# A one-core macaron layer: softplus on one activation table set, its last sum on GpSimd in the scans, and two batches of a layer norm on ScalarE

## The chip, the core and the metric

The kernel runs on one core of one Trainium2 chip. The core has TensorE (PE: matrix products; PEld is its weight load), VectorE (DVE), ScalarE (ACT), GpSimd (POOL) and SyncE (SP), which here only issues DMAs. The engines have a queue of instructions each and wait for each other by semaphores. The metric is the device time of one execution in microseconds; lower is better. Before the change the median of three runs is 441.34 us (440.18 to 441.75).

## The reference

Everything is float32. The input `x` has 4 batches of 512 tokens with 256 features.

```
x = x + 0.5 * ffn(layernorm(x))      # 8 experts, the best one per token, plus a shared expert
x = x + ssm(layernorm(x))            # a selective state space model
x = x + 0.5 * ffn(layernorm(x))      # the same weights again

ssm(x):  dt_x, B, C = split(x @ W_x.T, [64, 80])
         dt = softplus(dt_x @ W_dt.T + b_dt)
         for each of 16 states n, along the 512 tokens:
             h = exp(dt * A[:, n]) * h + dt * B[:, n] * x
             y += h * C[:, n]
         return y + x * D
```

The change concerns the middle line: how `softplus(z) = max(z, 0) + ln(1 + exp(-|z|))` is computed, and, beside the scans, the third `layernorm`.

## The kernel before

The features lie on the partitions: `[128, 2, 512]` is one batch, with 2 halves of 128 features. The program runs through the first ffn (to about 110 us), then projections and softplus of batch 0 (to 142.8 us), then 64 scans, four batches of 16 states (to 329.4 us), and then the second ffn. `s = 16 b + n` numbers the scans, and each engine has its own loop `scan(b)` over `n`, written out by hand; nothing reorders instructions. What a scan needs and gives:

- ACT makes `decay(s)`, `exp(dt * A)`, into `da` (L663), up to 3 scans ahead (`ahead`, AHEAD = 3). It waits for scan s - 4, since `da` and `hs` have RING = 4 buffers.
- The input term `dt * x * B` is made in one of two ways. For 42 of the 64 states ACT (`outer`, L679) and DVE (`outer`, L1405) multiply `dtx_t` by a column of B and PE turns the result into a PSUM bank (`turn_dbx`, L1030); the table BY_DVE gives how many of the 4 token tiles are DVE's, in 20 states at least one. For the other 22 states PE multiplies `dtx_t` by diagonal matrices of B (L1037). ACT reads B from `b_t` in SBUF, DVE reads it from `B_T` in the PSUM bank `Y`.
- DVE runs the scan itself (L1421): `da` from SBUF, the input term from PSUM, `hs` to SBUF.
- POOL multiplies `hs` by C into `gs` (L523, one product for each scan), and PE adds the products up in PSUM (`add`, L1054). In PE's loop `turn_dbx(s + 2)` stands ahead of `add(s - 1)`.
- After scan 1 of the next batch DVE adds the finished sum to `x_sb` (`add_y`, L1457). It waits for the `add` of the last state of its batch, and statistics of the third layer norm follow it (L1177). This is the narrow place between two batches.

Softplus of batch b + 1 is worked into the loop of batch b, on all engines: `project` (PE, L983), `project_copy` (ACT, L630), `project_z` (PE, L1003, one half of the features at a time, both into the PSUM bank `T`), `project_abs` (ACT: |z| and, L637, max(z, 0)), `project_exp` (ACT, L641), `project_u` (ACT, L650: 1 + w, with w = exp(-|z|)), `project_w` (DVE, L1370: the rounding error of 1 + w), `project_ln` (ACT, L657: ln(1 + w), with a table load before it and one after it, L663), `project_dt` (DVE, L1381 and L1384: two sums), `turn_dt` (PE, L1014), `project_dtx` (DVE, L1390). `project_bt` turns B (PE, L994) and copies it to SBUF (DVE, L1361). Batch 0 does the same ahead of the scans.

The third layer norm of batch b - 1 is worked into the loop of batch b as well: `rstd_of(2, b - 1)` on POOL, then four `normalise` instructions, on POOL (L469) for batches 0 and 1 and on ACT (L686) for batch 2; ACT takes a bias of -mean * rstd that POOL makes in `shift`. Batch 3's are on DVE, after the scans.

## Time and profile before

| | us |
|---|---|
| median of 3 runs | 441.34 |
| the profiled execution | 441.44 |
| its span, first to last instruction | 439.6 |
| PE busy in the span | 402.4 (92%) |
| DVE busy | 329.5 (75%) |
| POOL busy | 281.1 (64%) |
| ACT busy | 275.0 (63%) |

The 1.84 us between the span and the execution's time lie outside the first and last instruction. The granted TensorE clock is 0.996 of full speed over the span, so matrix products keep one price throughout. The shares are averages over stages with different limits; in the scans DVE, ACT and POOL are all busy most of the time, and the views below cut the span at the three `add_y` instructions (197.57, 244.19 and 289.39 us), so that one row is about one batch.

A row of the timeline has the start in us, the busy time in us, the engine, the line, the operation, output<-input, and in brackets how long the engine stood idle ahead of it and what ended that. A row of grouped instructions has the count, the busy sum in us and the mean in ns.

### The profile page before, as it was taken

What the parts mean: (1) busy time and instruction counts of PE and PEld (TensorE: products, weight loads), DVE (VectorE), ACT (ScalarE), POOL (GpSimd) and SP (SyncE); (2) the same over time, 40 slices, a digit from 0 to 9 for tenths busy, and PEclk for the clock granted to TensorE, in tenths of its full rate; (3) what the DMA queues carried; (4) which work ended last, traced back from release to release, by engine and by line L of the source; (5) the groups of instructions that cost most, each with busy time, mean ns of one, the idle gap of its engine ahead of it and who ended that gap; (6) DMA issues with size and microseconds to landing.
All of it is one profiled execution on the core that took longest, in us unless ns stands there. A gap on an engine that the chain in (4) does not pass through costs nothing. (4 is left out here: it accounts for less than half of the span.)

```text
span 439.6 us, 8329 instructions
## 1 busy us (share of the span) xinstructions
PE 402.4 (92%) x2716; PEld 278.4 (63%) x2716; DVE 329.5 (75%) x518; ACT 275.0 (63%) x501; POOL 281.1 (64%) x216
## 2 busy tenths in 40 slices
PE   6899899999996899899989997989999899899995
...
GB/s 250 385 179 264 48 54 167 284 174 101 204 10 91 73 82 180 81 144 106 186 75 118 141 176 73 115 157 92 121 72 0 172 107 120 99 118 135 111 60 48
DMA packets 50808, 56.84 MB, mean 129 GB/s; under 512 B 16329, under 2 KB 35597, under 8 KB 50768
## 3 DMA queue, kind: packets, MB, share of 16 engines
...
## 5 line engine op out<-in xcount | busy, mean ns | idle before, releaser
L523 POOL TENSOR_TENSOR gs<-hs,c_sb 128x1024 f32<-128x1024 f32 x63 | 148.3, 2380 | 18.7 <-DVE hs L1421 11.4
L1421 DVE TENSOR_TENSOR_SCAN hs<-da,bank 128x1024 f32<-128x1024 f32 x64 | 144.1, 2273 | 4.1 <-PE bank L1030 2.1
L663 ACT ACTIVATE da<-dt_sb,a_neg 128x511 f32<-128x511 f32 x128 | 84.5, 713 | 2.4 <-DVE dt_sb L1384 1.2
L1054 PE MATMUL bank<-ident,gs 128*128 128x128 f32 x504 | 66.3, 275 | 7.5 <-POOL gs L523 5.9
L1054 PEld LDWEIGHTS bank<-ident,gs 128*128 128x128 f32 x504 | 55.9, 141 | 12.1 <-POOL gs L523 9.8
L679 ACT ACTIVATE dbx_t<-dtx_t,h_sb 128x256 f32<-128x256 f32 x145 | 62.1, 498 | 1.6 <-DVE dtx_t L1390 1.4
L879 PE MATMUL bank<-xnT,w_gu 128*128 128x512 f32 x112 | 50.8, 601 | 0.0
L1030 PE MATMUL bank<-ident,dbx_t 128*128 128x128 f32 x336 | 44.2, 274 | 6.8 <-DVE hs L1421 4.1
L477 POOL DMA_INDIRECT da<-rows,row_token x29 | 30.6, 1055 | 29.7 <-DVE row_token L1292 21.2
L1030 PEld LDWEIGHTS bank<-ident,dbx_t 128*128 128x128 f32 x336 | 37.5, 141 | 12.2 <-DVE hs L1421 5.9
L591 ACT ACTIVATE th<-bank,da 128x256 f32<-128x256 f32 x36 | 17.0, 473 | 43.1 <-PE bank L918 30.4
L918 PE MATMUL bank<-w_gu,tt 128*128 x72 | 35.6, 616 | 3.2 <-ACT tt L596 2.2
L498 POOL DMA_INDIRECT token_out<-y_sb,row_token x18 | 19.0, 1056 | 29.2 <-DVE y_sb L1338 26.3
L477 POOL DMA_INDIRECT da<-rows,row_half x14 | 14.7, 1054 | 35.5 <-DVE row_token L1297 27.2
L1328 DVE TENSOR_TENSOR h_sb<-th,bank 128x256 f32<-128x256 f32 x36 | 15.1, 420 | 28.0 <-ACT th L591 27.9
L915 PE MATMUL bank<-w_gu,tt 128*32 x72 | 34.3, 598 | 1.4 <-ACT tt L596 1.4
L879 PEld LDWEIGHTS bank<-xnT,w_gu 128*128 128x128 f32 x112 | 21.0, 194 | 22.4 <-issue 22.3
L915 PE MATMUL bank<-dtx_t,tt 128*32 128x512 f32 x72 | 34.3, 598 | 0.0
L574 ACT ACTIVATE hs<-bank 128x512 f32<-128x512 f32 x10 | 6.0, 597 | 40.0 <-PE bank L879 34.6
L596 ACT ACTIVATE tt<-bank 128x512 f32<-128x512 f32 (+1 forms) x40 | 22.1, 553 | 13.6 <-PE bank L933 12.3
L498 POOL DMA_INDIRECT out<-y_sb,row_token x18 | 19.8, 1098 | 16.1 <-DVE y_sb L1341 8.2
L562 ACT ACTIVATE xnT<-bank 128x512 f32<-128x512 f32 x24 | 13.9, 590 | 17.3 <-PE bank L807 17.2
...
## 6 DMA issues: line engine op xcount, KB each, us to landing
...
```

What stands on the lines that cost most here:

```text
L477: nc.gpsimd.indirect_dma_start(out=xr[:, u, lo:hi], out_offset=None, in_=source, in_offset=bass.IndirectOffsetOnAxis(ap=row, axis=0), boun ...
L498: nc.gpsimd.indirect_dma_start(out=rows_back, out_offset=bass.IndirectOffsetOnAxis(ap=row_token[:, TILE[j]:TILE[j] + 1], axis=0), in_=y_sb ...
L523: nc.gpsimd.tensor_tensor(gs[:, s % 2], hs[:, s % RING], c_sb[:, s % RING].unsqueeze(1).to_broadcast([P, KC, L]), ALU.mult).then_inc(sc_g, 1)
L596: nc.scalar.activation(tt[:, (j + 1) % 2, lo:hi], T[:, lo * P:hi * P].rearrange("p (a t) -> p a t", t=P), ACT.Copy).then_inc(ff_tpc, 1)
L663: nc.scalar.activation(da[:, s % RING, k, 1:L], dt_sb[:, k, seq(s // N)][:, 1:L], ACT.Exp, scale=a_neg[:, k, s % N:s % N + 1]).then_inc(sc ...
L679: step = nc.scalar.activation(plain_buffer(s)[:, i, :], dtx_t[:, b % 2, i, :], ACT.Copy, scale=b_t[:, b, i, n:n + 1])
L879: last = nc.tensor.matmul(shared_banks(r, b, fo)[h], w_gu[:, k, SHARED, h * F + fo * P:h * F + (fo + 1) * P], xnT[:, k, b * L:(b + 1) * L] ...
L915: last = nc.tensor.matmul(H[j % 2][part, :], tt[:, j % 2, 2 + k, part], gu_part(i, g)[:, k, :] if g else w, start=(k == 0), stop=(k == KC ...
L918: last = nc.tensor.matmul(H[j % 2][:, :], tt[:, j % 2, 2 + k], w, start=(k == 0), stop=(k == KC - 1))
L1030: mm = nc.tensor.transpose(DBX[s % 2][:, k, i * P:(i + 1) * P], plain_buffer(s)[:, i, k * P:(k + 1) * P], ident[:])
L1054: mm = nc.tensor.matmul(YA[k][:, i * P:(i + 1) * P], products[:, k, i * P:(i + 1) * P], ident[:], start=(s % N == 0 and i == 0), stop=(s % ...
L1421: nc.vector.tensor_tensor_scan(hs[:, s % RING].rearrange(flat), da[:, s % RING].rearrange(flat), DBX[s % 2][:, :, :].rearrange(flat), 0.0, ...
```

## The change

Softplus: `project_u` becomes one ScalarE instruction over both halves that gives -(1 + w); it writes to SBUF (`neg_u`: half of `dtx_t` for batch 0, `y_sb` for the others) and no longer to PSUM. DVE adds 1 and w to it (`project_rest`, one instruction with both inputs in SBUF), then takes the larger of that and z + b_dt, which it reads from PSUM itself (`project_max`, two instructions); ScalarE's max(z, 0) goes. The last sum, with ln(1 + w), is one instruction (`project_dt`): on DVE for batch 0, on GpSimd in the scans. ScalarE loads the table set `natural_log_exp_and_others` ahead of the scans, so that Exp and Ln change no set; a load now stands ahead of the first Tanh in batch 3.

Banks: the two halves of z, and of `turn_dt`, go to `T` and `Y`, where both went to `T` before. `Y` also holds `B_T`, so `project_z` of the second half waits for the copy of B to SBUF, `project_bt` moves ahead, and DVE's `outer` reads `b_t` in SBUF in place of `B_T` in PSUM. `project_dtx` is one instruction in the scans.

Layer norm: for batches 0 and 1 `normalise` goes from GpSimd to ScalarE (n = 6 to 9), with a `shift` on GpSimd each.

```diff
...
-            return YA[k] if b == 0 else T
+            return (YA if b == 0 else (T, Y))[k]
+
+        def neg_u(b):
+
+            return dtx_t[:, 1].rearrange("p (k a) d -> p k (a d)", k=KC) if b == 0 else sg_h
...
+            def project_dt(b):
+                pool.wait_ge(pj_ln, b + 1)
+                pool.wait_ge(pj_max, KC * (b + 1))
+                nc.gpsimd.tensor_tensor(dt_sb[:, :, seq(b)], log_w, neg_u(b), ALU.add).then_inc(pj_dt, 1)
...
+                    if b < BATCH - 1 and n == 6 + int(b == 0):
+                        project_dt(b + 1)
...
                     if b > 0 and n == 3:
                         rstd_of(2, b - 1)
-                    if b == BATCH - 1 and n == 3:
+                    if b > 0 and n == 3:
                         shift(b - 1)
-                    if 0 < b < BATCH - 1 and 5 <= n < 5 + LT:
-                        normalise(2, b - 1, (n - 5,))
...
                 nc.scalar.activation(w_exp[:, k], pj_bank(b, k), ACT.Abs, bias=b_sb[:, k:k + 1]).then_inc(pj_abs, 1)
-                nc.scalar.activation(dt_sb[:, k, seq(b)], pj_bank(b, k), ACT.Relu, bias=b_sb[:, k:k + 1]).then_inc(pj_max, 1)
...
-            def project_u(b, k):
-
-                if k == 0:
-                    act.wait_ge(pj_exp, b + 1)
-                    act.wait_ge(pj_max, KC * (b + 1))
+            def project_u(b):
+
...
-                nc.scalar.activation(pj_bank(b, k), w_exp[:, k], ACT.Identity, bias=1.0).then_inc(pj_u, 1)
+                    act.wait_ge(pj_dt, b)
+                nc.scalar.activation(neg_u(b), w_exp[:], ACT.Identity, bias=neg_one[:, 0:1], scale=-1.0).then_inc(pj_u, 1)
...
                         project_exp(b + 1)
-                        project_u(b + 1, 0)
+                        project_u(b + 1)
                     if 0 < b < BATCH - 1 and n == 4 + late:
                         project_ln(b + 1)
                     if b == 0 and n == 15:
                         project_copy(2)
-                    if not more and 6 <= n < 6 + LT:
+                    if b > 0 and 6 <= n < 6 + LT:
                         normalise(b - 1, n - 6)
...
-            nc.scalar.preload_act_table(ACT.Exp)
+            nc.scalar.preload_act_table_set(EXP_LN)
...
             project_exp(0)
+            project_u(0)
             project_ln(0)
             shared_gate(0, 3, 1)
+            nc.scalar.preload_act_table_set(EXP_LN)
             act.wait_ge(a_ready, 2)
-            act.wait_ge(pj_dt, KC)
+            act.wait_ge(pj_dt, 1)
...
                 if b == 0:
                     pe.wait_ge(sh_hidden, 6)
                 else:
-                    pe.wait_ge(sc_dve, states_by("dve", N * (b - 1) + 4 + 3))
+                    pe.wait_ge(pj_btc, b)
...
                 if b > 0 and k > 0:
-                    pe.wait_ge(pj_max, KC * b + k)
+                    pe.wait_ge(pj_btc, b + 1)
...
-                pe.wait_ge(pj_dt, KC * (b + 1))
-                if b > 0 and h > 0:
-                    pe.wait_ge(pj_dtx, 2 * b + h)
-                dst = YA[h] if b == 0 else T
+                pe.wait_ge(pj_dt, b + 1)
+                dst = pj_bank(b, h)
...
-                    if more and n == 3:
+                    late = (2, 1, 0, 0)[b]
+                    if more and n == late:
                         project_bt(b + 1)
...
-                    if more and n - int(b == 0) in (8, 10):
-                        turn_dt(b + 1, (n - 8) // 2)
+                    if more and n - int(b == 0) in (8, 9):
+                        turn_dt(b + 1, n - int(b == 0) - 8)
...
-            def project_w(b, k):
-
-                if k == 0:
-                    dve.wait_ge(pj_exp, b + 1)
-                    dve.wait_ge(pj_max, KC * (b + 1))
-                if b > 0:
-                    dve.wait_ge(pj_u, KC * (b - 1) + k + 1)
-                    nc.vector.scalar_tensor_tensor(out=pj_bank(b, k), in0=pj_bank(b, k), scalar=1.0, in1=w_exp[:, k],
-                                                   op0=ALU.subtract, op1=ALU.subtract).then_inc(pj_rest, 1)
-                    return
-                nc.vector.tensor_scalar(pj_bank(b, k), w_exp[:, k], 1.0, -1.0, ALU.add, ALU.add).then_inc(pj_w, 1)
-                dve.wait_ge(pj_w, KC * b + k + 1)
-                nc.vector.tensor_tensor(pj_bank(b, k), w_exp[:, k], pj_bank(b, k), ALU.subtract).then_inc(pj_rest, 1)
...
-            def project_dt(b, k):
-
-                dve.wait_ge(pj_ln, b + 1)
-                dve.wait_ge(pj_rest, KC * b + k + 1)
-                nc.vector.tensor_tensor(pj_bank(b, k), log_w[:, k], pj_bank(b, k),
-                                        ALU.add if b == 0 else ALU.subtract).then_inc(pj_sum, 1)
-                dve.wait_ge(pj_sum, KC * b + k + 1)
-                nc.vector.tensor_tensor(dt_sb[:, k, seq(b)], pj_bank(b, k), dt_sb[:, k, seq(b)], ALU.add).then_inc(pj_dt, 1)
-
...
+            def project_rest(b):
+
+                dve.wait_ge(pj_u, b + 1)
+                nc.vector.scalar_tensor_tensor(out=neg_u(b), in0=neg_u(b), scalar=1.0, in1=w_exp[:],
+                                               op0=ALU.add, op1=ALU.add).then_inc(pj_rest, 1)
+
+            def project_max(b):
+
+                dve.wait_ge(pj_rest, b + 1)
+                for k in range(KC):
+                    nc.vector.scalar_tensor_tensor(out=neg_u(b)[:, k], in0=pj_bank(b, k), scalar=b_sb[:, k:k + 1], in1=neg_u(b)[:, k],
+                                                   op0=ALU.add, op1=ALU.max).then_inc(pj_max, 1)
+
+            def project_dt():
+
+                dve.wait_ge(pj_ln, 1)
+                dve.wait_ge(pj_max, KC)
+                nc.vector.tensor_tensor(dt_sb[:, :, seq(0)], log_w, neg_u(0), ALU.add).then_inc(pj_dt, 1)
...
+            def project_dtx(b):
+
+                halves = ((0, 1), (1, 2)) if b == 0 else ((0, 2),)
+                for lo, hi in halves:
+                    dve.wait_ge(pj_tp, 2 * b + hi)
+                    src = pair[3 if b == 0 else 1][:, lo:hi].rearrange("p h (i d) -> p (h i) d", d=D)
+                    nc.vector.tensor_tensor(dtx_t[:, b % 2, 2 * lo:2 * hi], src, xn[:, LT * b + 2 * lo:LT * b + 2 * hi, :],
+                                            ALU.mult).then_inc(pj_dtx, hi - lo)
...
+                    dve.wait_ge(pj_btc, b + 1)
                 nc.vector.tensor_tensor(plain_buffer(s)[:, LT - mine:, :], dtx_t[:, b % 2, LT - mine:, :],
-                                        B_T[:, b, LT - mine:, n:n + 1].to_broadcast([P, mine, D]), ALU.mult).then_inc(sc_dve, 1)
+                                        b_t[:, b, LT - mine:, n:n + 1].to_broadcast([P, mine, D]), ALU.mult).then_inc(sc_dve, 1)
...
-                    if more and n == 4:
+                    late = int(b == 0)
+                    if more and n == (3, 2, 1)[b]:
                         project_bt(b + 1)
-                    late = int(b == 0)
-                    if more and n in (5 + late, 7 + late):
-                        project_w(b + 1, (n - 5) // 2)
-                    if more and n in (6 + late, 8 + late):
-                        project_dt(b + 1, (n - 6) // 2)
-                    if more and n in (10 + late, 12 + late):
-                        project_dtx(b + 1, (n - 10) // 2)
+                    if more and n == 5 + late:
+                        project_rest(b + 1)
+                    if more and n == 6 + late:
+                        project_max(b + 1)
+                    if more and n == 11 + late:
+                        project_dtx(b + 1)
...
```

What stands in a queue now, at three places.

PE in batch 0, from the addition of the first product to the transposition that scan 5 needs (`bank2` is `T`, `bank0` and `bank4` are the banks of the input term, `bank6` is the sum). Before:

```order
L1054 MATMUL bank6<-ident,gs 128x128 x8
L983 MATMUL bank2<-xnT,w_x 96x512 x2
L1030 MATMUL bank0<-ident,dbx_t 128x128 x8
L1054 MATMUL bank6<-ident,gs 128x128 x8
L1003 MATMUL bank2<-th,w_dt 128x512
L994 MATMUL bank2<-ident,th 128x16 x4
L1030 MATMUL bank4<-ident,dbx_t 128x128 x8
```

And now:

```order
L1066 MATMUL bank6<-ident,gs 128x128 x8
L997 MATMUL bank2<-xnT,w_x 96x512 x2
L1008 MATMUL bank2<-ident,th 128x16 x4
L1042 MATMUL bank0<-ident,dbx_t 128x128 x8
L1066 MATMUL bank6<-ident,gs 128x128 x8
L1017 MATMUL bank2<-th,w_dt 128x512
L1042 MATMUL bank4<-ident,dbx_t 128x128 x8
```

`project_bt` (L994, now L1008) stood behind the transposition for scan 4 and behind `project_z`; now it is the first thing behind `project(1)`, and the transposition for scan 4 (bank0) waits behind it. `project_bt` waits for ScalarE's copy of what `project(1)` gave. In batch 2 it stands in the same place behind `project(3)`, ahead of the transposition for scan 34 and of the last `add` of batch 1, for which `add_y(1)` waits.

DVE in batch 1, from scan 20 (n = 4) to scan 24; rows with `hs<-da` are scans. Before:

```order
L1421 SCALAR_TENSOR_TENSOR hs<-da,bank0 128x1024
L1361 COPY h_sb<-bank2 128x64
L1421 SCALAR_TENSOR_TENSOR hs<-da,bank4 128x1024
L1370 SCALAR_TENSOR_TENSOR bank2<-bank2,w_exp 128x512
L1421 SCALAR_TENSOR_TENSOR hs<-da,bank0 128x1024
L1381 TENSOR_TENSOR bank2<-tt,bank2 128x512
L1384 TENSOR_TENSOR dt_sb<-bank2,dt_sb 128x512
L1421 SCALAR_TENSOR_TENSOR hs<-da,bank4 128x1024
L1370 SCALAR_TENSOR_TENSOR bank2<-bank2,w_exp 128x512
L1405 TENSOR_TENSOR dbx_t<-dtx_t,bank2 128x256
L1421 SCALAR_TENSOR_TENSOR hs<-da,bank0 128x1024
```

And now, with B's copy ahead of scan 19 (no row here):

```order
L1432 SCALAR_TENSOR_TENSOR hs<-da,bank0 128x1024
L1432 SCALAR_TENSOR_TENSOR hs<-da,bank4 128x1024
L1378 SCALAR_TENSOR_TENSOR y_sb<-y_sb,w_exp 128x1024
L1432 SCALAR_TENSOR_TENSOR hs<-da,bank0 128x1024
L1385 SCALAR_TENSOR_TENSOR y_sb<-bank2,b_sb,y_sb 128x512 x2
L1432 SCALAR_TENSOR_TENSOR hs<-da,bank4 128x1024
L1416 TENSOR_TENSOR dbx_t<-dtx_t,h_sb 128x256
L1432 SCALAR_TENSOR_TENSOR hs<-da,bank0 128x1024
```

Two `project_w` and four sums became one `project_rest` over 1024 elements, with both inputs in SBUF, and two `project_max`. The `outer` (`dbx_t<-dtx_t`) read `bank2` (`B_T`); that of state 26 here reads `h_sb`, where `b_t` lies, now.

POOL in batch 1, from the statistics' rstd on. Before:

```order
L454 TENSOR_SCALAR var_eps<-mv 128x4
L455 TENSOR_TENSOR rstd<-var_eps,neg_half 128x4
L523 TENSOR_TENSOR gs<-hs,c_sb 128x1024 x2
L469 TENSOR_SCALAR xn_no<-x_sb,mv,rstd 128x256
L523 TENSOR_TENSOR gs<-hs,c_sb 128x1024
L469 TENSOR_SCALAR xn_no<-x_sb,mv,rstd 128x256
L523 TENSOR_TENSOR gs<-hs,c_sb 128x1024
L469 TENSOR_SCALAR xn_no<-x_sb,mv,rstd 128x256
L523 TENSOR_TENSOR gs<-hs,c_sb 128x1024
L469 TENSOR_SCALAR xn_no<-x_sb,mv,rstd 128x256
L523 TENSOR_TENSOR gs<-hs,c_sb 128x1024 x11
```

And now:

```order
L461 TENSOR_SCALAR var_eps<-mv 128x4
L462 TENSOR_TENSOR rstd<-var_eps,neg_half 128x4
L469 TENSOR_TENSOR mean_rstd<-mv,rstd 128x4
L470 TENSOR_SCALAR mean_rstd<-mean_rstd 128x4
L537 TENSOR_TENSOR gs<-hs,c_sb 128x1024 x3
L526 TENSOR_TENSOR dt_sb<-tt,y_sb 128x2x512
L537 TENSOR_TENSOR gs<-hs,c_sb 128x1024 x13
```

The four `normalise` between the products went; two short instructions of `shift` and one sum over 1024 elements (`dt_sb<-tt`) came. In batch 0 POOL keeps its `normalise` and gets the sum as well. On ACT the four `normalise` stand from n = 6 to 9, between the decays and outers of the states 25 to 28.

## Rows read from the trace of the kernel before

**Rows 1.** Windows: busy us (and count) by engine, granted clock, DMA share, GB/s.

```profile
142.80:197.60 54.80, 50.47 (x391) 44.19 (x390) 50.56 (x47) 48.96 (x91) 47.76 (x24) 1.00 0.44 111
163.30:195.30 32.00, 29.25 (x244) 26.76 (x243) 30.41 (x25) 30.21 (x55) 31.75 (x17) 1.00 0.57 132
197.60:244.20 46.60, 43.99 (x353) 38.64 (x352) 45.11 (x42) 44.00 (x82) 43.81 (x23) 1.00 0.49 127
244.20:289.40 45.20, 41.67 (x345) 37.86 (x346) 43.92 (x39) 42.46 (x79) 42.33 (x22) 1.00 0.42 126
289.40:332.20 42.80, 40.96 (x325) 38.22 (x324) 38.90 (x35) 32.62 (x68) 35.66 (x19) 1.00 0.33 99
```

**Rows 2.** Timeline, DVE: the three additions between two batches.

```profile
197.57 1.28 DVE L1457 TENSOR_TENSOR x_sb<-x_sb,bank 128x512 f32<-128x512 f32 x2 [0.51 <-PE bank L1054]
...
244.19 1.28 DVE L1457 TENSOR_TENSOR x_sb<-x_sb,bank 128x512 f32<-128x512 f32 x2 [0.83 <-PE bank L1054]
...
289.39 1.28 DVE L1457 TENSOR_TENSOR x_sb<-x_sb,bank 128x512 f32<-128x512 f32 x2 [1.18 <-PE bank L1054]
```

**Rows 3.** Groups: busy us, mean ns of one, idle us before them and releasers.

```profile
L523 POOL TENSOR_TENSOR gs<-hs,c_sb 128x1024 f32<-128x1024 f32 x63 | 148.3, 2380 | 18.7 <-DVE hs L1421 11.4 <-PE bank L1054 7.1
...
L1421 DVE TENSOR_TENSOR_SCAN hs<-da,bank 128x1024 f32<-128x1024 f32 x64 | 144.1, 2273 | 4.1 <-PE bank L1030 2.1 <-PE bank L1037 2.0
...
L469 POOL TENSOR_SCALAR xn_no<-x_sb,mv,rstd 128x256 f32<-128x256 f32 x20 | 24.4, 1226 | 0.0
...
L1384 DVE TENSOR_TENSOR dt_sb<-bank,dt_sb 128x512 f32<-128x512 f32 x8 | 5.5, 691 | 0.3
...
L657 ACT ACT_TABLE_LOAD x4 | 5.1, 1283 | 0.1
...
L1357 DVE TENSOR_TENSOR x_sb<-xn_no,x_sb 128x1024 f32<-128x1024 f32 x3 | 3.7, 1222 | 2.7 <-DMA xn_no<-token_out 2.7
...
L650 ACT ACTIVATE bank<-w_exp 128x512 f32<-128x512 f32 x6 | 3.6, 595 | 0.5 <-DVE dt_sb L1384 0.4
...
L1405 DVE TENSOR_TENSOR dbx_t<-dtx_t,bank 128x256 f32<-128x256 f32 x17 | 6.8, 402 | 0.1
...
L686 ACT ACTIVATE xn_no<-x_sb,mean_rstd,rstd 128x256 f32<-128x256 f32 x4 | 2.4, 593 | 0.0
...
L512 POOL TENSOR_TENSOR x_sb<-xn_no,x_sb 128x1024 f32<-128x1024 f32 x1 | 2.2, 2176 | 0.0
```

**Rows 4.** Timeline, PE: the first transposition of dt of batch 0.

```profile
137.57 1.09 PE L1014 MATMUL bank<-ident,dt_sb 128*128 128x128 f32 x8 [1.05 <-DVE dt_sb L1384]
```

**Rows 5.** Timeline, DVE: two waits in batch 0.

```profile
168.03 0.70 DVE L1381 TENSOR_TENSOR bank<-tt,bank 128x512 f32<-128x512 f32 x1 [0.68 <-ACT tt L657]
...
172.38 0.70 DVE L1370 SCALAR_TENSOR_TENSOR bank<-bank,w_exp 128x512 f32<-128x512 f32 x1 [0.74 <-ACT bank L650]
```

**Rows 6.** Timeline, PE: what follows project(1) in batch 0.

```profile
153.96 1.04 PE L1030 MATMUL bank<-ident,dbx_t 128*128 128x128 f32 x8
...
156.85 0.42 PE L994 MATMUL bank<-ident,th 16*128 16x16 f32 x4
```

**Rows 7.** Timeline, ACT: two copies of projections, the outer of state 50.

```profile
154.16 0.59 ACT L630 ACTIVATE th<-bank 96x512 f32<-96x512 f32 x1 [2.26 <-PE bank L983]
...
242.68 0.58 ACT L630 ACTIVATE th<-bank 96x512 f32<-96x512 f32 x1
...
285.53 1.71 ACT L679 ACTIVATE dbx_t<-dtx_t,h_sb 128x256 f32<-128x256 f32 x4
```

**Rows 8.** Timeline, PE: the transposition for scan 50.

```profile
287.34 1.07 PE L1030 MATMUL bank<-ident,dbx_t 128*128 128x128 f32 x8 [0.32 <-issue]
```

**Rows 9.** Line L1450 alone: duration ns min/median/max, first and last start us.

```profile
L1450 DVE TENSOR_TENSOR dbx_t<-hs,c_sb x2: 678/968/1259, 329.4 to 330.6; 128x512 f32<-128x512 f32 x2
```

**Rows 10.** Timeline, DVE and POOL: that line, and the last product on POOL.

```profile
329.42 1.86 DVE L1450 TENSOR_TENSOR dbx_t<-hs,c_sb 128x512 f32<-128x512 f32 x2
...
327.78 2.35 POOL L523 TENSOR_TENSOR gs<-hs,c_sb 128x1024 f32<-128x1024 f32 x1 [0.52 <-PE bank L1054]
```

46 lines of the change are left out of this document (22 added, 24 removed).

## The prediction

> **What bounds the kernel now.** I read the windows first, cut at the three `add_y`, since the whole-span shares mix stages. In the three windows that hold batches 0 to 2, DVE is busy 50.56 of 54.80, 45.11 of 46.60 and 43.92 of 45.20 us; POOL and ACT each stand at 87 to 94%, PE at 92 to 94%, at a granted clock of 1.00 [rows 1]. So DVE comes first, with two engines close behind, and each may be the last somewhere. The change touches only these batches and the 15 us ahead of them; the second ffn behind them is shifted as a whole.
>
> Then I looked at where DVE waits. The places that matter are the `add_y`: DVE stands idle 0.51, 0.83 and 1.18 us ahead of them, for PE's last `add` [rows 2]. These three starts (197.57, 244.19, 289.39) are my milestones: what moves the third moves the end, because statistics, scan 51 and PE's queue follow it, and PE is busy 40.96 of the next 42.80 us [rows 1]. Between milestones I ask which engine is last; a saving on another one is lost there.
>
> Third, whether POOL has room: from 163.3 to 195.3 us it is busy 31.75 of 32.00 us [rows 1]. In that stretch anything added to POOL comes out at its end.
>
> **The change, part by part.** All terms are against the profiled execution (441.44 us, span 439.6, 1.84 outside). It stands 0.1 above the median of the runs, so I add the sum to 441.34.
>
> *Ahead of the scans.* Behind Exp the old chain has four DVE instructions of `project_w` and four sums, 8 x 0.69 [rows 3], and PE's first transposition of dt starts at 137.57, 1.05 idle for DVE [rows 4]. The new chain loses the two maxima ahead of Exp (one of them was beside PE's second half of z, so 0.6), and has after it u (1024 elements: 2 x 0.595 [rows 3] less the 0.1 by which neighbours overlap, as 1.28 for a pair [rows 2] against 2 x 0.69 shows: 1.09), `project_rest` (1.22, by L1357 of the same size [rows 3]), two `project_max` (2 x 0.69) and the sum (1.22): 4.9 against 5.5. Together -1.1 us. The table load that Ln loses comes back behind Tanh; it ends about when dt is ready, and costs nothing.
>
> *To milestone 0.* (a) `project_bt` stands right behind `project(1)`, and waits for ACT's copy, which `project(1)` released at 154.16 and which ended at 154.75 [rows 7]; then come its own 0.42 [rows 6]. The transposition for scan 4, which began at 153.96 [rows 6], begins at about 155.2: +1.26. Queued behind it are that transposition, the `add` of product 1 and z, and scan 4 waits for it. The 0.42 come back where it stood, so +0.85 stays. (b) POOL gets the sum, 2.18 by L512, an addition of the same size [rows 3], bounded above by the 2.38 of a product. POOL is full there, with 0.25 us free in the 32 [rows 1]: +1.9. (c) What DVE saves here (the waits of 0.68 and 0.74 [rows 5], and 1.4 of work, below) is lost, as POOL is last. Milestone 0: -1.1 + 0.85 + 1.9 = +1.65.
>
> *To milestone 1.* DVE loses 2 `project_w`, 4 sums and 2 `project_dtx` (8 x 0.69 = 5.5) and gets 1.22 + 2 x 0.69 + 1.22 = 3.8 in half as many instructions, each of which overlaps the one before by 0.1: -1.4. POOL loses four `normalise` (4 x 1.23 [rows 3]), gets 2.18 and a short `shift`: -2.7, and it is no longer last. But before `add_y(1)` PE does `project(3)`, the transposition for scan 34 and the `add`, and now `project_bt` between them, with its wait for the copy: 0.6 + 0.42, +1.05. That copy ran at 242.68 right behind other work of ACT, with no wait [rows 7]; ACT now has four `normalise` (0.59 each, 0.5 with the overlap [rows 3]) in its fullest stretch, and what it loses (maxima, a load of 1.28 before Ln and one after) lies in the first third, where it may not run ahead of the ring of four. I take +1.0. Milestone 1: +1.65 - 1.4 + 2.05 = +2.3.
>
> *To milestone 2.* DVE -1.4 again, POOL again -2.7. ACT's `outer` of state 50 ends at 287.24 [rows 7] and PE's transposition starts at 287.34 [rows 8], so ACT is last together with POOL; with ACT later by up to 1.0 the net lies between -1.4 and +1.0, and I take -0.4. Behind it the load for Tanh, 1.28 [rows 3], stands mostly in ACT's lead: +0.35.
>
> Without anything else the sum is +2.25, 443.6.
>
> *Two inputs from SBUF.* This is what decides. DVE's 20 `outer`, four `project_rest` and the one sum on DVE now read two tiles from SBUF, beside a POOL that reads SBUF all the time. The kernel before has one such place in the scans: the last product, `hs` times `c_sb`, twice the same shape. It took 1259 ns once and 678 the other time [rows 9]. The slow one started at 329.42, while POOL ran its last product from 327.78 to 330.13; the fast one ran with POOL idle [rows 10]. DVE operations of that size with one input in PSUM take 691 under a busy POOL [rows 3]. So the price shown is 0.58 an instruction. At 23 of the 25 POOL is busy (at the `outer` of states 3 and 5 it waits for others): 23 x 0.58 = 13.3. Hidden are DVE's idle at the milestones, 2.5 [rows 2], and as much again that the terms above leave, as POOL, PE or ACT is last there: 5.0. Net +8.3. The bounds: 0, if an input that repeats one number along 256 elements or if `outer`, which stands right behind a scan, mostly comes ahead of the product that waits for the same scan; below 0 it can't go, since no instruction gets shorter. Above, a wait for the whole rest of POOL's instruction, half a product or 1.2 at a place where the two don't run in step. I take the 0.58, the one row.
>
> The Trainium skill ("SBUF — State Buffer", "Who interferes with whom") says that a Vector instruction with two SBUF inputs and a GpSimd instruction that reads SBUF exclude each other for the whole of the one that came first. By it 0.58 is only the rest of the one product that [rows 10] happens to show, and the price is the rest of whatever POOL is at; that is the second rival below. Nothing above rests on it.
>
> **Sum.** +2.25 + 8.3 = +10.6: 452.0 us.
>
> **The rivals.** About 0.5%, 2.2 us, is what a measurement of this kernel can tell from no change.
>
> 1. No price for the second SBUF input, at least for an `outer` that repeats one column. For: the two operands of [rows 9] are full tiles, and there are only two instructions. Against: nothing in the rows tells that a repeated column is read elsewhere. Time: the terms without it, 443.6, on the edge of no change (439.1 to 445.5).
> 2. The whole wait. Once DVE has waited for POOL's end, scan (2.27) and product (2.38) run nearly in step [rows 3] and the next wait is short, so only the heads pay: five ahead of the scans at half a `normalise` (3.0), three `project_rest` (3.6) and some ten `outer` (12) at half a product: 18.6 less 5.0 hidden. 441.3 + 2.25 + 13.6 = 457.
> 3. Faster: the engine totals decide. DVE is busiest in each window [rows 1]; its savings of 3 x 1.4, the waits of 1.42 and the start of 1.1 come to -6.7: 434.6. It needs POOL's sum and PE's wait for the copy to find room, and no price for SBUF. For: DVE's 92 to 97%. Against: POOL's 31.75 of 32.00 and the `add_y` waits [rows 1, 2]. It decides from the point where milestone 0 is earlier than 197.57.
> 4. The change doesn't do what it says: a table load stays between Exp and Ln. It would add back 2.6 us of ACT in each batch, but the order shows no load there; under 1 in 100.
>
> **How the numbers follow.** Forecast (446 to 456): 0.43. Rival 2 (456 and above): 0.13. Rival 1: 0.27, of it 0.17 within 0.5% and 0.10 above. Rival 3: 0.17, rival 4 in it. So slower 0.43 + 0.13 + 0.10 = 0.66, same 0.17, faster 0.17. The likeliest case's own range is 446 to 456. The range that leaves out 0.2 goes from 440.0, with rival 3 below it, to 459.0, with the end of rival 2 above.
>
> **What would show it.** In the profile after: `outer` on DVE, 402 ns for one tile before [rows 3], with a mean near 0.9 us and a maximum above 1.5; `project_rest` above 1.22; if they stay at 0.4 and 1.2, the price is not there and the largest term is wrong. POOL's sum at 2.2 to 2.4 behind product 7, and `add_y(0)` later than 197.57; earlier would refute the terms of milestone 0. PE idle for ACT's copy at `project_bt`, 0.6 us in batches 0 and 2. No table load between scans 0 and 47, one of 1.28 at the first Tanh. DVE's idle ahead of `add_y(1)` longer than 0.83.

## The result and the profile after

The changed kernel takes 453.65 us (median of four runs, 452.3 to 455.0): 1.0289 times the kernel before, with a 95% interval of 1.0243 to 1.0336. The profiled execution is one of the two longer ones: 455.0, span 453.3, so 13.7 more than the span of before. Of the runs below, one of the six of g2_psum_bt (477.77, granted clock 0.849) was slow and is left out of its median and ratio. The windows, cut as in [rows 1] at the three `add_y` (one stretch of batch 0 and the whole of each batch):

```profile
142.90:206.40 63.50, 54.64 (x388) 46.43 (x387) 53.53 (x42) 45.50 (x85) 51.77 (x26) 0.92 0.37 94
...
153.00:159.00 6.00, 5.38 (x12) 2.62 (x12) 2.72 (x3) 0.33 (x1) 2.34 (x1) 0.50 0.01 3
...
206.40:256.70 50.30, 45.58 (x358) 40.73 (x356) 47.53 (x38) 42.75 (x81) 43.72 (x22) 0.97 0.49 130
256.70:302.80 46.10, 41.00 (x342) 37.64 (x343) 44.79 (x35) 40.30 (x77) 42.89 (x21) 1.00 0.42 116
302.80:345.90 43.10, 40.94 (x325) 38.22 (x324) 38.99 (x35) 33.92 (x69) 34.53 (x19) 1.00 0.31 94
```

Batch 0 is 8.7 longer than in [rows 1], batch 1 3.7, batch 2 0.9, and the rest 0.3. No engine became full; all of them wait more (a wait of DVE beside POOL, below, counts as DVE's busy time). In batch 0 the granted clock averages 0.92, and in six microseconds it is 0.50, the lower of its two levels (1.2 GHz); two shorter stretches at half clock follow, in batches 0 and 1. The three additions, beside [rows 2], with DVE's idle ahead of them:

```profile
206.44 1.29 DVE L1468 TENSOR_TENSOR x_sb<-x_sb,bank 128x512 f32<-128x512 f32 x2 [0.77 <-PE bank L1066]
256.67 1.28 DVE L1468 TENSOR_TENSOR x_sb<-x_sb,bank 128x512 f32<-128x512 f32 x2 [2.24 <-PE bank L1066]
302.77 1.28 DVE L1468 TENSOR_TENSOR x_sb<-x_sb,bank 128x512 f32<-128x512 f32 x2 [0.81 <-PE bank L1066]
```

The groups that answer to [rows 3] (L1416 is DVE's `outer`, L1378 `project_rest`, L526 POOL's new sum, L537 its product, L478 its `normalise`, L598 the first Tanh):

```profile
L537 POOL TENSOR_TENSOR gs<-hs,c_sb 128x1024 f32<-128x1024 f32 x63 | 151.5, 2428 | 26.8 <-PE bank L1066 15.4 <-DVE hs L1432 11.1
L478 POOL TENSOR_SCALAR xn_no<-x_sb,mv,rstd 128x256 f32<-128x256 f32 x12 | 16.7, 1401 | 0.0
L1416 DVE TENSOR_TENSOR dbx_t<-dtx_t,h_sb 128x256 f32<-128x256 f32 x17 | 16.2, 953 | 0.0
L526 POOL TENSOR_TENSOR dt_sb<-tt,y_sb 128x1024 f32<-128x1024 f32 x3 | 7.5, 2489 | 0.0
L1378 DVE SCALAR_TENSOR_TENSOR y_sb<-y_sb,w_exp 128x1024 f32<-128x1024 f32 x3 | 4.3, 1425 | 0.0
L598 ACT ACT_TABLE_LOAD x1 | 1.3, 1283 | 0.0
```

`outer` of one tile went from 402 to 953 ns. Its longest one shows how batch 0 lost its time. DVE, POOL and PE in turn, from behind scan 1 to scan 4:

```profile
147.62 0.66 DVE L1315 SCALAR_TENSOR_TENSOR x_sb<-bank,x_sb 128x512 f32<-128x512 f32 x1
148.20 2.22 DVE L1416 TENSOR_TENSOR dbx_t<-dtx_t,h_sb 128x256 f32<-128x256 f32 x1
150.34 2.27 DVE L1432 TENSOR_TENSOR_SCAN hs<-da,bank 128x1024 f32<-128x1024 f32 x1
...
159.77 0.22 DVE L1373 COPY h_sb<-bank 128x64 f32<-128x64 f32 x1 [4.05 <-PE bank L1008]
160.80 2.29 DVE L1432 TENSOR_TENSOR_SCAN hs<-da,bank 128x1024 f32<-128x1024 f32 x1 [0.80 <-PE bank L1042]
...
147.78 2.36 POOL L537 TENSOR_TENSOR gs<-hs,c_sb 128x1024 f32<-128x1024 f32 x1
...
153.25 1.97 PE L1066 MATMUL bank<-ident,gs 128*128 128x128 f32 x8 [3.68 <-DVE x_sb L1315]
155.01 3.62 PE L997 MATMUL bank<-xnT,w_x 128*96 128x512 f32 x4
159.32 0.41 PE L1008 MATMUL bank<-ident,th 16*128 16x16 f32 x4 [0.68 <-ACT th L644]
```

The `outer` of state 4 starts while POOL's product runs (147.78 to 150.14) and ends at 150.42, 0.28 behind it. Scan 2 and the next addition to `x_sb` are 2 us late, so PE stands idle for 3.68. Then comes the first stretch at half clock: the eight transpositions of `add` in 1.97 (1.09 at full clock) and `project(1)` in 3.62 (1.88 at full clock), 2.6 lost. `project_copy`, `project_bt` and DVE's copy of B hang on `project(1)`, and scan 4 starts 5.77 later than the 155.03 of before; counted from scan 0, that is 5.6 of the 8.7.

### The profile page after: what moved, and what is told of

Read it like the earlier page. It is cut to its first block and busy times, and to the rows that moved or that the text cites. A ratio compares the mean times of both kernels' runs of the same rounds, so it can differ in the third digit from the quotient of the medians.

```text
span 453.3 us, 8300 instructions
## 1 busy us (share of the span) xinstructions
PE 407.3 (90%) x2716; PEld 282.7 (62%) x2716; DVE 334.7 (74%) x502; ACT 269.7 (60%) x494; POOL 285.8 (63%) x216
## 5 line engine op out<-in xcount | busy, mean ns | idle before, releaser
L537 POOL TENSOR_TENSOR gs<-hs,c_sb 128x1024 f32<-128x1024 f32 x63 | 151.5, 2428 | 26.8 <-PE bank L1066 15.4
L1066 PE MATMUL bank<-ident,gs 128*128 128x128 f32 x504 | 68.4, 280 | 11.4 <-POOL gs L537 7.7
L1066 PEld LDWEIGHTS bank<-ident,gs 128*128 128x128 f32 x504 | 58.3, 144 | 15.4 <-POOL gs L537 11.4
L1042 PE MATMUL bank<-ident,dbx_t 128*128 128x128 f32 x336 | 45.8, 281 | 9.2 <-DVE hs L1432 5.6
L1042 PEld LDWEIGHTS bank<-ident,dbx_t 128*128 128x128 f32 x336 | 38.8, 144 | 13.6 <-DVE hs L1432 8.5
L507 POOL DMA_INDIRECT out<-y_sb,row_token x18 | 18.7, 1038 | 16.7 <-DVE y_sb L1353 9.3
L576 ACT ACTIVATE xnT<-bank 128x512 f32<-128x512 f32 x24 | 13.9, 589 | 17.9 <-PE bank L821 17.9
```

What stands on the lines that cost most here:

```text
L507: nc.gpsimd.indirect_dma_start(out=rows_back, out_offset=bass.IndirectOffsetOnAxis(ap=row_token[:, TILE[j]:TILE[j] + 1], axis=0), in_=y_sb ...
L537: nc.gpsimd.tensor_tensor(gs[:, s % 2], hs[:, s % RING], c_sb[:, s % RING].unsqueeze(1).to_broadcast([P, KC, L]), ALU.mult).then_inc(sc_g, 1)
L1042: mm = nc.tensor.transpose(DBX[s % 2][:, k, i * P:(i + 1) * P], plain_buffer(s)[:, i, k * P:(k + 1) * P], ident[:])
L1066: mm = nc.tensor.matmul(YA[k][:, i * P:(i + 1) * P], products[:, k, i * P:(i + 1) * P], ident[:], start=(s % N == 0 and i == 0), stop=(s % ...
```

## Experiments

The stretches ahead of scan 0 and behind batch 2 differ between the profiles by themselves (scan 0 starts between 141.0 and 145.6, and 150.2 to 152.2 follow the third `add_y`). So beside the times I compare the lengths of the batches, from scan 0 and from `add_y` to `add_y`, of one profile for each kernel. A ratio is to the kernel before in the same series of runs, whose median was 440.8 to 441.7:

| kernel | median us | ratio to before (95%) | batch 0 | 1 | 2 | sum |
|---|---|---|---|---|---|---|
| before | 441.3 | | 54.79 | 46.62 | 45.20 | 146.61 |
| changed | 453.65 | 1.0289 (1.0243 to 1.0336) | 63.53 | 50.23 | 46.10 | 159.86 |
| e2_before_sbuf | 454.11 | 1.0294 (1.0275 to 1.0314) | 63.48 | 48.62 | 46.93 | 159.03 |
| e8_before_set | 441.70 | 0.9996 (0.9977 to 1.0014) | 54.79 | 46.60 | 45.24 | 146.63 |
| e1_scalar | 451.55 | 1.0228 (1.0197 to 1.0260) | 62.09 | 48.18 | 45.72 | 155.99 |
| e3_bt_back | 454.77 | 1.0309 (1.0291 to 1.0328) | 62.37 | 50.99 | 46.10 | 159.46 |
| e4_outer4 | 449.57 | 1.0218 (1.0168 to 1.0269) | 58.79 | 48.67 | 46.12 | 153.58 |
| f1_none | 453.37 | 1.0270 (1.0228 to 1.0312) | 58.25 | 51.41 | 45.47 | 155.13 |
| f4_none_bt | 450.01 | 1.0158 (1.0113 to 1.0204) | 57.80 | 47.95 | 46.06 | 151.81 |
| f3_halves | 460.58 | 1.0423 (1.0389 to 1.0456) | 66.96 | 49.47 | 46.84 | 163.27 |
| g1_psum | 448.48 | 1.0148 (1.0120 to 1.0177) | 58.72 | 47.65 | 45.20 | 151.57 |
| g2_psum_bt | 445.96 | 1.0117 (1.0086 to 1.0149) | 57.87 | 47.09 | 45.19 | 150.15 |
| g3_psum_bt_norm | 451.72 | 1.0231 (1.0202 to 1.0261) | 57.88 | 49.74 | 48.61 | 156.23 |
| g4_best | 445.20 | 1.0083 (1.0052 to 1.0114) | 55.57 | 47.09 | 45.19 | 147.85 |

**One part alone: `outer` reads `b_t` (e2_before_sbuf).**

```diff
                 if n == 0:
                     dve.wait_ge(pj_dtx, 2 * (b + 1))
+                    dve.wait_ge(pj_btc, b + 1)
...
-                                        B_T[:, b, LT - mine:, n:n + 1].to_broadcast([P, mine, D]), ALU.mult).then_inc(sc_dve, 1)
+                                        b_t[:, b, LT - mine:, n:n + 1].to_broadcast([P, mine, D]), ALU.mult).then_inc(sc_dve, 1)
```

> The kernel before with one part of the change alone: DVE's outer reads b_t in SBUF in place of B_T in PSUM, and waits for b_t once in each batch. Theory: outer of 128x256 goes from a mean of 402 ns to 0.8 to 1.0 us with a maximum near 2; 17 x 0.5 = 8.5 and the six tiles ahead of the scans, of which about half is hidden in DVE's waits: 4 to 9 more than before, 445 to 450. Rival A (the path lies elsewhere): outer is as long, and the time within 1.5 of before. Rival B (it is the order of the changed kernel that makes DVE and POOL meet): outer's mean stays below 0.6.

This one operand brings as much as the whole change: +12.8 us, more than I had expected. `outer` of one tile has a mean of 1127 ns. In the profile, each long `outer` ends 0.28 to 0.29 behind the end of an instruction of POOL. The rows stand by engine, not in order of time. The first three are DVE's: two `outer`, and the two scans behind the one at 185.38; the others are POOL's instructions at those places:

```profile
231.74 1.64 DVE L1406 TENSOR_TENSOR dbx_t<-dtx_t,h_sb 128x256 f32<-128x256 f32 x1
...
185.38 4.60 DVE L1406 TENSOR_TENSOR dbx_t<-dtx_t,h_sb 128x256 f32<-128x256 f32 x1
189.90 4.45 DVE L1422 TENSOR_TENSOR_SCAN hs<-da,bank 128x1024 f32<-128x1024 f32 x2
...
230.73 2.36 POOL L523 TENSOR_TENSOR gs<-hs,c_sb 128x1024 f32<-128x1024 f32 x1
233.08 1.39 POOL L469 TENSOR_SCALAR xn_no<-x_sb,mv,rstd 128x256 f32<-128x256 f32 x1
...
185.02 4.67 POOL L523 TENSOR_TENSOR gs<-hs,c_sb 128x1024 f32<-128x1024 f32 x2
...
187.35 2.34 POOL L523 TENSOR_TENSOR gs<-hs,c_sb 128x1024 f32<-128x1024 f32 x1
```

At 231.74 DVE waits for the product's end (233.09) and goes in ahead of POOL's `normalise`, which takes 1.39 in place of 1.22. At 185.38 it waits past the first of two products (185.02 to 187.36) and past the second, which ends at 189.69. POOL's products keep their usual length meanwhile (2.36 and 2.34). So it is a wait, not a rate that the two share.

**The table set alone (e8_before_set).**

```diff
-            nc.scalar.preload_act_table(ACT.Exp)
+            nc.scalar.preload_act_table_set(EXP_LN)
```

> The kernel before with one part of the change alone: the table set that holds Exp and Ln is loaded in place of the one for Exp. ACT loses two loads of 1.28 us in each of four batches, and gets one behind Tanh. Theory (batch 0's ahead of the scans lies on the path, the others on ACT beside DVE and POOL, which end last): 1 to 2 less, 439 to 440.5. Rival (ACT is last ahead of add_y, so that each load counts): 4 to 6 less, 435 to 437.

No change, 0.9996; but the experiment is inconclusive, since the edit was too small. Its profile still has the loads in the scans, ahead of Ln and behind it, three each:

```profile
L658 ACT ACT_TABLE_LOAD x3 | 3.8, 1283 | 0.1
L664 ACT ACT_TABLE_LOAD x3 | 3.8, 1283 | 0.1
```

One of the four ahead of Ln is gone, the one ahead of the scans ([rows 3]: four). The changed kernel asks for the set a second time, behind the gate of the shared expert, and this one does not. So it shows only that the load ahead of the scans was worth nothing; what the six in the scans are worth was not measured.

**`outer` with one tensor from SBUF (e1_scalar).**

```diff
-                nc.vector.tensor_tensor(plain_buffer(s)[:, LT - mine:, :], dtx_t[:, b % 2, LT - mine:, :],
-                                        b_t[:, b, LT - mine:, n:n + 1].to_broadcast([P, mine, D]), ALU.mult).then_inc(sc_dve, 1)
+                for i in range(LT - mine, LT):
+                    step = nc.vector.tensor_scalar(plain_buffer(s)[:, i, :], dtx_t[:, b % 2, i, :], b_t[:, b, i, n:n + 1], None, ALU.mult)
+                step.then_inc(sc_dve, 1)
```

> The changed kernel, with DVE's outer written as one tensor_scalar per tile: the column of b_t goes in as a scalar for each partition, so that dtx_t is the one tensor that it reads from SBUF. All else stays. Theory (an instruction of DVE with two tensors from SBUF waits for POOL's running instruction): outer of 128x256 falls from a mean of 953 ns to about 400, none above 0.6; add_y(0) comes about 6 us earlier than 206.44 since the 2.22 us outer of state 4, PE's idle of 3.68 behind it and the stretch at half clock go; the time falls by 8 to 10, to 443 to 446. Rival A (the moved project_bt and ACT's and POOL's added work make the loss, and the long outer lie beside other waits): outer shortens too, but the time stays above 450. Rival B (any read of b_t from SBUF beside POOL is slow, as a scalar too): outer keeps its mean near 0.9 and the time stays at 452 to 455.

My theory missed by 6 us; the mean fell and the time stayed above 450, as rival A has it. Alone the instruction is faster than before, 0.32 (145.07), but beside POOL it waits all the same (the second row):

```profile
145.07 0.32 DVE L1417 TENSOR_SCALAR dbx_t<-dtx_t,h_sb 128x256 f32<-128x256 f32 x1
...
148.09 2.08 DVE L1417 TENSOR_SCALAR dbx_t<-dtx_t,h_sb 128x256 f32<-128x256 f32 x1
```

The group of all 23 tiles:

```profile
L1417 DVE TENSOR_SCALAR dbx_t<-dtx_t,h_sb 128x256 f32<-128x256 f32 x23 | 15.7, 698 | 0.1
```

So a second tensor in SBUF is not the only thing that makes DVE wait. Whether it is a faster mode or the scalar, this run does not tell.

**`project_bt` back behind the add (e3_bt_back).**

```diff
-                    if more and n == late:
-                        project_bt(b + 1)
                     if s + 2 < STATES:
                         turn_dbx(s + 2)
...
+                    if more and n == late:
+                        project_bt(b + 1)
                     if more and n in (late, late + 1):
                         project_z(b + 1, n - late)
```

> The changed kernel, with PE's project_bt behind the transposition for scan s+2 and the add, just ahead of z, in place of ahead of them. Theory (project_bt costs its wait for ACT's copy, 0.68 us idle and 0.41, in batch 0, up to 1 again in batch 1; the rest of the loss is the outer): the transposition for scan 4 no longer waits for the copy; 1 to 3 us less than the changed kernel, 450 to 453. Rival (in batch 0 scan 4 starts 5.77 later than before, and all of that hangs on project_bt standing behind a project(1) at half clock): 5 to 6 us less, 446 to 449.

Neither: no gain (454.77); in the profile batch 0 is 1.2 shorter and batch 1 0.8 longer. DVE's copy of B still waits, 4.06 for the slow `project(1)`, and the three `project_rest` now meet POOL at another time (mean 2236 ns against 1425; the one in batch 1 took 3399).

**The one long `outer` to ACT (e4_outer4).**

```diff
-    BY_DVE = ((2, 2, 2, 1, 1, 1) + ...
+    BY_DVE = ((2, 2, 2, 1, 0, 1) + ...
```

> The changed kernel, with the outer of state 4 wholly on ACT (four tiles in place of three and one on DVE). Theory (this one instruction, 2.22 us in place of 0.41, makes PE idle for 3.68 us, and behind that idle PE's granted clock is 0.50 from 153 to 159 us): PE's idle there falls to about 1.6, its clock stays at 1.00, scan 4 starts about 4 us earlier than 160.80, and the time is 3 to 6 less than the changed kernel's, 448 to 450. Rival (the next outer, of state 5, or another place takes over the wait): 452 to 455 as before the edit.

As the theory has it: 449.57, though its four runs spread from 448.1 to 453.6 and the profile is of the shortest. The clock in batch 0 is 1.00, scan 4 starts 13.2 behind scan 0 (17.9 in the changed kernel, 12.3 before), and batch 0 is 4.7 shorter.

**All `outer` from state 4 on to ACT, and `project_bt` back in that kernel (f1_none, f4_none_bt).**

```diff
-    BY_DVE = ((2, 2, 2, 1, 1, 1) + (0,) * 6 + (1, 0, 1, 0),) + ...
+    BY_DVE = ((2, 2, 2, 1) + (0,) * 12,) + ((0,) * 16,) * 3
```

> The changed kernel, with DVE's outer given to ACT in all states from 4 on (16 tiles; DVE keeps the seven of states 0 to 3). Theory (the long outer make the loss; each ends 0.28 to 0.29 us behind the end of an instruction of POOL, so they wait for the whole of it): DVE loses 16 us of outer, ACT gets 16 x 0.5 = 8 us, 2 to 4 in a batch, and has lost two table loads and two maxima (4 us) in each; PE's granted clock stays at 1.00; 440 to 444, and below 441 if ACT has the room. Rival (ACT with its four normalise becomes the bound): add_y(1) and add_y(2) come later by 3 each than without; 447 to 450.

> The kernel without DVE's outer from state 4 on, and with PE's project_bt behind the transposition and the add, just ahead of z. Theory (project_bt ahead of the transposition costs PE's wait for ACT's copy and its own 0.4, in each of three batches, where nothing else is late): 1 to 3 us less than the same kernel with project_bt where the change put it; 438 to 442. Rival (the later bt copy on DVE holds z(1), and so the whole chain of dt): no change, or 1 more.

f1_none took the rival's way, and farther: 453.37. No `outer` beside the scans waits for POOL any more (`project_rest` does, 3195 ns in batch 1), but DVE now waits for PE, and PE for ACT. DVE's idle ahead of `add_y(1)` is the longest of all kernels, and ahead of it PE waits at `project_bt` for ACT's copy:

```profile
252.84 1.28 DVE L1468 TENSOR_TENSOR x_sb<-x_sb,bank 128x512 f32<-128x512 f32 x2 [5.51 <-PE bank L1066]
...
250.49 0.42 PE L1008 MATMUL bank<-ident,th 16*128 16x16 f32 x4 [2.90 <-ACT th L644]
```

ACT makes that copy at 249.85, behind `outer` of four tiles each and with no idle time since 237.6: those tiles stand on DVE where ACT has no room. In this kernel `project_bt` moved back gives 3.4 us, to 450.01, not the 438 to 442 expected (batch 1: 51.41 to 47.95), where in e3_bt_back it gave nothing: the worth of an order depends on what else is late.

**POOL's product in two halves (f3_halves).**

```diff
-                    nc.gpsimd.tensor_tensor(gs[:, s % 2], hs[:, s % RING], c_sb[:, s % RING].unsqueeze(1).to_broadcast([P, KC, L]), ...
+                    for k in range(KC):
+                        part = nc.gpsimd.tensor_tensor(gs[:, s % 2, k], hs[:, s % RING, k], c_sb[:, s % RING], ALU.mult)
+                    part.then_inc(sc_g, 1)
```

> The changed kernel, with POOL's product of 128x1024 issued as two of 128x512. Theory (DVE waits for the end of POOL's running instruction): the longest outer behind a product falls from 2.2 to about 1.5, as the half product ends after 1.2, or DVE goes in between the two; the mean of 128x256 falls from 953 ns to 600 to 700. 63 more instructions on POOL cost it something that no row shows, 0.05 to 0.15 each, so the time falls by less: 446 to 452. Rival (the two only share a rate while they run side by side): the durations stay, mean 0.95, and the time is 453 or more.

The theory was wrong; of the rival the time came true (453 or more), but not its reason. The kernel is the slowest of all. Its `outer` have a mean of 1173 ns, but that hangs on a single one: the other 16 have 852, below the 953 of the changed kernel. The cut also costs POOL itself 7.3 us over all products (158.8 in place of 151.5), 0.12 each; no row stood behind the 0.05 to 0.15 expected. The longest `outer`, and POOL's series beside it:

```profile
191.43 6.32 DVE L1417 TENSOR_TENSOR dbx_t<-dtx_t,h_sb 128x256 f32<-128x256 f32 x1
...
187.57 9.88 POOL L538 TENSOR_TENSOR gs<-hs,c_sb 128x512 f32<-128x512 f32 x8
...
191.27 6.18 POOL L538 TENSOR_TENSOR gs<-hs,c_sb 128x512 f32<-128x512 f32 x5
```

DVE waited for five half products, 191.27 to 197.45, and ended 0.30 behind the last. Shorter instructions of POOL need not let DVE in between them when they stand back to back. (The one at 148.54, the 2.22 of the changed kernel, took 1.19 and came in after one half.) When a following instruction lets DVE go first stays open.

**`outer` with its second tensor in PSUM (g1_psum), `project_bt` back (g2_psum_bt), and `normalise` back on POOL (g3_psum_bt_norm).** The second tensor is a piece of the bank of scan s - 2, which the second operation ignores. So `outer` also waits until that bank is filled, as the scan behind it must anyway. The states 0 to 2 keep the old form:

```diff
...
+                dve.wait_ge(sc_dbx, s - 1)
+                nc.vector.scalar_tensor_tensor(out=plain_buffer(s)[:, LT - 1, :], in0=dtx_t[:, b % 2, LT - 1, :],
+                                               scalar=b_t[:, b, LT - 1, n:n + 1], in1=DBX[s % 2][:, 0, 0:D],
+                                               op0=ALU.mult, op1=ALU.bypass).then_inc(sc_dve, 1)
```

> The changed kernel, with DVE's outer from state 3 on written as a scalar_tensor_tensor: dtx_t from SBUF, the column of b_t as a scalar for each partition, and as second tensor a piece of the bank of the scan before last, in PSUM, which the second operation (bypass) does not use. All else stays. Theory (two tensors in SBUF, or a faster mode, are what makes DVE wait for POOL; with the second in PSUM it does not, as the L1405 of before): outer of 128x256 back at 0.39 to 0.45 us, none above 0.6; PE's idle of 3.68 at 153 us back near 1.6 and its clock at 1.00; the loss of 12.8 that the one part alone brought goes, and what is left is the rest of the change: 441 to 445. Rival A (the read of b_t as a scalar beside POOL waits): outer's mean 0.7 as with the tensor_scalar, 450 to 452. Rival B (the moves of POOL's sum, of the normalise and of project_bt lose as much): outer short, and 448 or more.

> The same, and PE's project_bt behind the transposition for scan s+2 and the add, just ahead of z. Theory: PE's wait for ACT's copy and 0.4 of its own go out of the path in batch 0 at least: 1 to 3 us below the kernel with the second input in PSUM alone; 439 to 442. Rival (z(1), which now waits for the later bt copy, holds up the chain of dt): the same time, or up to 1 more.

> The same as the one with project_bt moved back, and POOL, not ACT, normalises batches 0 and 1 again, as before the change. Theory (in batches 1 and 2 ACT has taken 2.4 us and POOL has lost 4.9 against a sum of 2.4; POOL has no room, ACT a little): 1 to 4 us more. Rival (ACT's four normalise make PE wait for ACT's outer at the ends of batches 1 and 2, as where ACT got all outer): 1 to 3 us less.

The wait of these `outer` is gone, with `b_t` still read in SBUF as a scalar: a scalar from SBUF does not by itself make DVE wait. (That leaves a faster mode of `tensor_scalar` for e1_scalar; no run shows it by itself.) But the time fell to 448.48, not to 441 to 445: rival B is right as well. What is left stands in batch 0 (3.9 above before) and batch 1 (1.0); a part of it is still contention, since `project_rest` with its two tensors in SBUF took 1871 ns in batch 0 (1198 without a wait). `outer` alone (ns min/median/max, then first and last start), and behind it PE around scan 12:

```profile
L1421 DVE SCALAR_TENSOR_TENSOR dbx_t<-dtx_t,h_sb,bank x17: 449/471/482, 144.8 to 279.8; 128x256 f32<-128x256 f32 x17
```

```profile
180.52 1.97 PE L1066 MATMUL bank<-ident,gs 128*128 128x128 f32 x8 [2.06 <-POOL gs L537]
182.28 1.06 PE L1026 MATMUL bank<-ident,dt_sb 128*128 128x128 f32 x4
183.14 1.39 PE L1042 MATMUL bank<-ident,dbx_t 128*128 128x128 f32 x8
```

PE waits 2.06 for a product that stands behind POOL's new sum and a `normalise`, and runs at half clock after it, and the transposition for scan 12 is late. `project_bt` moved back gives 0.85 in batch 0 and 0.56 in batch 1, and 445.96 in place of the 439 to 442 expected. With `normalise` on POOL again, the time is 5.8 longer (1 to 4 were expected) and batches 1 and 2 are 2.65 and 3.42 longer: that part of the change is a gain, as long as POOL has the sum.

**The best of it (g4_best): g2_psum_bt, and in batch 0 alone the sum on DVE with its logarithm in PSUM, and the copy of B one scan later.** ACT's logarithm for batch 1 moves behind the maxima as well.

```diff
+                if b == 1:
+                    act.wait_ge(pj_max, 2 * KC)
-                nc.scalar.activation(log_w, w_exp[:], ACT.Ln, bias=1.0)
+                nc.scalar.activation(pair[1][:] if b == 1 else log_w, w_exp[:], ACT.Ln, bias=1.0)
...
-                    if b == 0 and n == 6:
-                        project_ln(1)
...
+                    if b == 0 and n == 8:
+                        project_ln(1)
...
-                    if b < BATCH - 1 and n == 6 + int(b == 0):
+                    if 0 < b < BATCH - 1 and n == 6:
                         project_dt(b + 1)
...
-                    if more and n == (3, 2, 1)[b]:
+                    if more and n == (4, 2, 1)[b]:
                         project_bt(b + 1)
...
+                    if b == 0 and n == 9:
+                        project_dt(1)
```

> The kernel with the second input in PSUM and project_bt moved back, and two edits in batch 0 alone: DVE makes the sum of dt for batch 1, behind scan 9, with the logarithm written to PSUM by ACT (behind the maxima), so that POOL has no sum there; and DVE's copy of b_t stands one scan later, behind scan 4 as before the change. Theory (what is left of the loss lies in batch 0, 57.9 us against 54.8: POOL is full from 158.9 to 191.9, its sum of 2.36 makes PE idle for 2.05 and then run at half clock from 180 to 185; and DVE's copy waited 2.41 for PE): batch 0 shrinks by 3 to 4, to 54 to 55; 442 to 444, at or just above the kernel before. Rival A (the sum on DVE, 1.22, and PE's turn behind it are as late as POOL's): no more than 1 less, 446. Rival B (with that gone the rest of the change shows as a gain): 438 to 440, faster than the kernel before.

Batch 0 is 2.3 shorter (55.57), and the theory's 54 to 55 and 442 to 444 were missed by about one. The sum takes DVE its 1.20 with one tensor in PSUM, while `project_rest` of batch 1 still waits for a product of POOL (211.34 to 213.71), for which it came 0.04 too late:

```profile
175.72 1.20 DVE L1394 TENSOR_TENSOR dt_sb<-bank,y_sb 128x1024 f32<-128x1024 f32 x1
...
211.38 3.41 DVE L1380 SCALAR_TENSOR_TENSOR y_sb<-y_sb,w_exp 128x1024 f32<-128x1024 f32 x1
...
211.34 2.37 POOL L537 TENSOR_TENSOR gs<-hs,c_sb 128x1024 f32<-128x1024 f32 x1
```

445.20 is 0.8% above before (1.0083, from 1.0052): no version here beats the kernel before. It undoes `outer` and part of the moves; what it keeps (one table set, fewer instructions on DVE, `normalise` on ACT) gives nothing that shows, as 45.19 against 45.20 in batch 2 says. It also keeps `project_rest` with two tensors from SBUF, which took 2250 and 3407 ns in batches 0 and 1 against 1198 in batch 2. What the rest of the change is worth with one of them in PSUM, as `project_w` had it, was not run, so the part of the loss that is not contention stays open.

## Why the prediction was right, step by step

Slower, by contention on SBUF: right, and 452.0 against 453.65; but the sum came near partly by luck, as two errors met. The terms against the batch lengths of the profiles, where "without contention" is g1_psum, in which `outer` no longer waits (`project_rest` still does):

| term | forecast | measured |
|---|---|---|
| start of the scans | -1.1 | +0.1 |
| batch 0 without contention | +2.75 | +3.93 |
| batch 1 without contention | +0.65 | +1.03 |
| batch 2 without contention | -0.4 | 0.00 |
| behind it (Tanh) | +0.35 | +0.32 |
| contention, net | +8.3 | +8.29 (changed less g1_psum); 5.2 by the medians |

The 8.29 is one profile against another, and the changed kernel's is one of its longer executions. By the medians the contention of `outer` costs 5.2, where 8.3 was forecast, and everything else 7.1 (g1_psum above before), where 2.25 was. The +0.32 shows nothing either: in g1_psum, with the same load, the stretch behind the third `add_y` is 2.0 longer than before.

- *What bounds.* The `add_y` as milestones held: the batches carry all of the loss, and the stretch behind them 0.3.
- *The start.* Wrong. The sum was ready at 136.68, 0.8 earlier than before (by its own terms the forecast was -1.2, not -1.1), but the first transposition of dt began at 137.47, against 137.57 [rows 4]. PE was late itself: it waited 1.37 for POOL's `normalise`, as the first row shows. One of POOL's started at 132.67, 0.02 behind DVE's `project_rest`, whose inputs both lie in SBUF; it and the next took 3.45, where two take 2.44 in the kernel before. The wait works in both directions, and I had priced only DVE's side.

```profile
134.97 0.66 PE L821 MATMUL bank<-ident,xn_no 128*128 128x128 f32 x4 [1.37 <-POOL xn_no L478]
...
132.67 3.45 POOL L478 TENSOR_SCALAR xn_no<-x_sb,mv,rstd 128x256 f32<-128x256 f32 x2
...
132.65 1.26 DVE L1378 SCALAR_TENSOR_TENSOR dtx_t<-dtx_t,w_exp 128x1024 f32<-128x1024 f32 x1 [1.82 <-ACT dtx_t L665]
```

- *`project_bt`.* PE waits 0.68 for the copy in batch 0, as said (0.6), and 1.08 in batch 2. +0.85 was forecast for batch 0, and g1_psum to g2_psum_bt gives 0.85 back. For batch 1 +1.05 was forecast: DVE's idle ahead of `add_y(1)` goes from 2.08 in g1_psum to 0.77 in g2_psum_bt, and 0.56 of that reaches the batch. The +1.0 for ACT's four `normalise` was not measured by itself.
- *POOL's sum.* 2.37 in batch 0, forecast 2.18 to 2.38; the longer ones of batches 1 and 2 (2.55) have an `outer` of DVE ahead of them. +1.9 was forecast; taking it away, with the copy of B, gives 2.3 (g4_best). That PE runs at half clock behind its wait for it was not foreseen.
- *`normalise`.* The -2.7 was POOL's busy time, four `normalise` less the sum, and stood in no milestone. g3_psum_bt_norm, with the sum and `normalise` both on POOL, is 2.65 and 3.42 longer in batches 1 and 2: another quantity, so the likeness of the numbers confirms nothing, but POOL had no room for both.
- *Two inputs from SBUF.* The term was near, its working was not. The step that failed is the price: 0.58 for each of 23 instructions, from the one slow row [rows 9, 10]. That row already was a wait: the slow instruction began at 329.42 and ended 1.26 later, at 330.68, 0.55 behind the end of POOL's product (330.13). It is not a price for each instruction. Ten of the 17 `outer` take 0.39 to 0.64; the other seven, 1.19 to 2.22, wait until a POOL instruction has ended, and end 0.28 behind it (up to 4.60 in e2_before_sbuf). That is the second rival's mechanism. Of the three `project_rest` in the scans one is above the 1.22 named as a sign (1.88); two take 1.20. The lengthening is 17 x (953 - 402) = 9.4 for `outer`, and some 1.0 for the other instructions, 10.4 in place of 13.3. What no term held is the half clock behind PE's waits: 2.6 us of PE in the first stretch, about 1.4 and 1.7 in two more. The four executions fit that: two at a mean clock of 0.981 take 454.9 and 455.0, two at 0.992 take 452.3 and 452.4. With `outer` alone changed the loss is 12.4, with the rest alone 5.0 (g1_psum), with both 13.3: the losses lie partly on each other, 4.1, where the forecast hid 5.0.

The Trainium skill ("SBUF — State Buffer", "Who interferes with whom") says that whichever of the two starts first holds the other off for its whole instruction. The rows agree as to the wait, on both sides; past one instruction (4.60 over two products, 6.32 over five halves) they go beyond it. By the same section `tensor_scalar` can enter a mode that takes the shared ports; the 0.32 and the waits of e1_scalar agree.

- *The rivals.* No price (443.6; the upper end of no change is 443.5, not 445.5): refuted by e2_before_sbuf, and by 953 ns. The whole wait: right as a mechanism; its sum, 457, was too high: it supposed 18.6 us of waits, and 10.4 came. Engine totals: refuted, milestone 0 is later. The table load stays: refuted, in the scans only Tanh's is left.

Open: what the six table loads in the scans are worth by themselves; what decides whether DVE gets in between two instructions of POOL; what the stretches at half clock are worth by themselves (in e4_outer4 the first goes together with the 2.22 that led to it); what `project_rest` would cost with one tensor in PSUM; and why the stretches outside the scans differ by 2 to 5 us between profiles.
